# Full attention: the fourth head's first scores a key tile later, peaks of three heads one maximum later

## The reference, cut to what matters

```python
k = jnp.repeat(k, G, axis=2)
v = jnp.repeat(v, G, axis=2)
scale = 1.0 / jnp.sqrt(jnp.float32(HD)).astype(q.dtype)
scores = jnp.einsum('bthd,bshd->btsh', q, k) * scale
probs = jax.nn.softmax(scores, axis=2)
context = jnp.einsum('btsh,bshd->bthd', probs, v).reshape(b, t, DIM)
```

## Time and profile before

| what | value |
|---|---|
| median of 3 runs | 3688.42 us (3686.24 to 3691.95) |
| the profiled execution, its own time | 3693.39 us |
| its span | 3691.6 us |
| PE busy over the span | 3270.0 us (89%) |
| DVE busy | 2747.2 us (74%) |
| ACT busy | 2229.4 us (60%) |
| POOL busy | 954.3 us (26%) |
| first to last score of this stage (line 1824) | 1883.5 to 3299.0 us |

### The profile page before, as it was taken

One profiled execution on the slowest core, in us unless ns is written; L12 is line 12 of the kernel. 1 busy time (PEld: TensorE's weight loads), 2 busy tenths in 40 slices (PEclk: granted clock), 3 DMA queues, 4 the chain that ended last, 5 costly groups with the idle time before them and its releaser, 6 DMA issues. The chain is left out here.

```text
span 3691.6 us, 55325 instructions
## 1 busy us (share of the span) xinstructions
PE 3270.0 (89%) x18162; PEld 1635.2 (44%) x18162; DVE 2747.2 (74%) x4130; ACT 2229.4 (60%) x3970; POOL 954.3 (26%) x906
## 2 busy tenths in 40 slices
PE   7848888997899978996679999999999999977996
PEld 3326777776566646773312222222222222214664
DVE  6639999998566654444688888888888888835665
ACT  5659999998000002221248888888888888862432
POOL 7529999996000000001300000000000000001000
PEclk9979999999899989998879999999999999998998
DMA  4447443321211136313210000000000010011001
GB/s 131 164 139 184 126 104 95 101 58 39 91 54 55 38 68 154 80 46 103 87 25 14 22 14 21 14 21 14 22 14 21 15 24 14 9 34 42 23 23 46
DMA packets 218533, 216.73 MB, mean 59 GB/s; under 512 B 63954, under 2 KB 164434, under 8 KB 217492
## 3 DMA queue, kind: packets, MB, share of 16 engines
q1 hardware_dynamic: 218276, 213.41, 20.9%
HBM read 145.99 MB, written 67.37 MB: 58 GB/s over the span
## 5 line engine op out<-in xcount | busy, mean ns | idle before, releaser
L1720 DVE TENSOR_REDUCE attn_part_max<-attn_pM 128x1 f32<-128x1024 f32 x1024 | 1204.9, 1219 | 161.7 <-PE attn_pM L1775 158.5
L1700 ACT ACTIVATE attn_probs<-attn_pE 128x512 f32<-128x512 f32 x2048 | 1089.8, 597 | 205.4 <-PE attn_pE L1824 200.9
L1824 PE MATMUL attn_pE<-attn_q,attn_k_exp 128*128 128x512 bf16 x2048 | 628.5, 385 | 31.6 <-ACT attn_q L1672 24.7
L535 POOL TENSOR_TENSOR scan_dbu<-scan_du,scan_b_all 128x2048 f32<-128x2048 f32 x128 | 578.2, 4549 | 15.0 <-DVE scan_h L594 13.2
L1795 PE MATMUL attn_pA<-attn_probs,attn_v 128*32 128x512 f32 x4096 | 560.3, 604 | 0.0
L594 DVE TENSOR_TENSOR_SCAN scan_h<-scan_abar,scan_states,scan_dbu 128x512 f32<-128x512 f32 x384 | 458.5, 1290 | 0.0
L1824 PEld LDWEIGHTS attn_pE<-attn_q,attn_k_exp 128*128 128x128 bf16 x2048 | 139.0, 97 | 608.5 <-ACT attn_probs L1700 464.7
L608 PE MATMUL scan_hT<-scan_ident,scan_h 128*128 128x128 f32 x2048 | 327.4, 284 | 68.0 <-ACT scan_hcT L546 26.0
L559 ACT ACTIVATE scan_abar<-scan_delta,scan_decay 128x512 f32<-128x512 f32 x512 | 374.7, 732 | 17.5 <-DVE scan_h L594 17.4
L546 ACT ACTIVATE scan_hcT<-scan_hT,scan_c_t 128x512 f32<-128x512 f32 x512 | 370.0, 723 | 1.2 <-PE scan_hT L608 1.1
L1653 POOL TENSOR_TENSOR attn_peak_parts<-attn_peak,attn_zero 128x4 bf16<-128x4 f32 x128 | 26.3, 205 | 1277.5 <-DVE attn_peak L1724 1277.5
(11 more groups left out here) (274 smaller groups left out, 3637.3 us busy)
## 6 DMA issues: line engine op xcount, KB each, us to landing
scan_b_all<-mid_BC SPq DMA_DIRECT2D x32, 1024.0 KB, 10.3
causal_rwB<-mid_rwT SPq DMA_DIRECT2D x64, 256.0 KB, 4.3
attn_q<-mid_q_parts SPq DMA_DIRECT2D x224, 64.0 KB, 2.4
mid_gT<-front_gT SPq DMA_DIRECT2D x8, 1024.0 KB, 7.6
mid_uT<-front_uT SPq DMA_DIRECT2D x8, 1024.0 KB, 9.2
mid_dT<-front_dT SPq DMA_DIRECT2D x8, 1024.0 KB, 4.3
scan_delta<-mid_dT SPq DMA_DIRECT2D x8, 1024.0 KB, 8.0
scan_u_in<-mid_uT SPq DMA_DIRECT2D x8, 1024.0 KB, 10.4
```

The source lines that it names most:

```text
L535: nc.gpsimd.tensor_tensor(dbu[:, G % NDBU, :, :], du[:, u % 2, :, :], b_row, ALU.mult).then_inc(dbu_ready, 1)
L1700: nc.scalar.activation(probs[:, kt % 4, h, :], pE[:, bank(item), :], ACT.Exp, scale=SCALE).then_inc(exp_done, 1)
L1720: nc.vector.reduce_max(part_max[:, h, j, i:i + 1], pM[:, m % 2, :], AXIS_X).then_inc(max_read, 1)
L1824: nc.tensor.matmul(pE[:, bank(item), :], k_exp[:, par, kt * 128:(kt + 1) * 128], q[:, qc, h, :], start=True, stop=True).then_inc(e_psum, 1)
```

## The change

Two things. First, the item list: head 3's score of tile 0 moves out of tile 0. Tile 0 now has the scores of heads 0 to 2 only; tile 1 has the row of head 3, its own heads 0 to 2, and then head 3 of tile 0 and head 3 of tile 1. In PE's order the sums of tile 14 of the unit before now end tile 0 (they stood in front of the row there as well), the row opens tile 1, and the sums of tile 15 stand in front of the two scores of head 3. The values that semaphores are compared with follow the new order (E_COUNT, KT_COUNT).

Second, DVE takes the peak of heads 0 to 2 not behind the head's last maximum, but behind the first maximum of the next head; the fourth head's stays where it was. A head's first maximum now also waits until the peak of the unit before has been taken (peak_ready), as it overwrites what that reads.

```diff
--- before.py
+++ after.py
@@ -1503,7 +1503,9 @@
     def step_items(kt):
 
         if kt == 0:
-            return [("e", 0), ("e", 1), ("e", 2), ("row", G - 1), ("e", 3)]
+            return [("e", h) for h in range(G - 1)]
+        if kt == 1:
+            return [("row", G - 1)] + [("e", G + h) for h in range(G - 1)] + [("e", G - 1), ("e", 2 * G - 1)]
         items = [("e", kt * G + h) for h in range(G)]
         if kt == OUT_KT:
             items.insert(3, ("out",))
@@ -1513,6 +1515,9 @@
 
     UNIT = [item for kt in range(KT) for item in step_items(kt)]
     P_UNIT = len(UNIT)
+    E_ORDER = [item[1] for item in UNIT if item[0] == "e"]
+    E_COUNT = {e: i + 1 for i, e in enumerate(E_ORDER)}
+    KT_COUNT = [max(E_COUNT[kt * G + h] for h in range(G)) for kt in range(KT)]
     assert P_UNIT % EB == 0
 
     def gone(item, start, end):
@@ -1693,11 +1698,11 @@
                                 if gone(item, start, end):
                                     continue
                                 if item[0] == "e":
-                                    h = item[1] % G
-                                    act.wait_ge(e_psum, u * E_UNIT + item[1] + 1)
+                                    e_kt, h = item[1] // G, item[1] % G
+                                    act.wait_ge(e_psum, u * E_UNIT + E_COUNT[item[1]])
                                     if h == 0:
                                         at_least(act, pv_done, u * KT + kt - 3)
-                                    nc.scalar.activation(probs[:, kt % 4, h, :], pE[:, bank(item), :], ACT.Exp, scale=SCALE).then_inc(exp_done, 1)
+                                    nc.scalar.activation(probs[:, e_kt % 4, h, :], pE[:, bank(item), :], ACT.Exp, scale=SCALE).then_inc(exp_done, 1)
                                 elif item[0] == "row":
                                     move_row(of_unit(item, u), qc if item[1] == G - 1 else (qc + 1) % QC, item[1])
                                 else:
@@ -1717,11 +1722,14 @@
 
                     h, j, i = m // M_HEAD, m % M_HEAD // 2, m % 2
                     dve.wait_ge(m_psum, u * M_UNIT + m + 1)
+                    if j == 0 and i == 0:
+                        at_least(dve, peak_ready, (u - 1) * G + h + 1)
                     nc.vector.reduce_max(part_max[:, h, j, i:i + 1], pM[:, m % 2, :], AXIS_X).then_inc(max_read, 1)
-                    if m % M_HEAD == M_HEAD - 1:
-                        dve.wait_ge(max_read, u * M_UNIT + m + 1)
-                        at_least(dve, parts_ready, (u - 1) * G + h + 1)
-                        nc.vector.tensor_reduce(peak[:, h, :], part_max[:, h, :, :], AXIS_X, ALU.max, negate=True).then_inc(peak_ready, 1)
+
+                def take_peak(h, u):
+                    dve.wait_ge(max_read, u * M_UNIT + (h + 1) * M_HEAD)
+                    at_least(dve, parts_ready, (u - 1) * G + h + 1)
+                    nc.vector.tensor_reduce(peak[:, h, :], part_max[:, h, :, :], AXIS_X, ALU.max, negate=True).then_inc(peak_ready, 1)
 
                 def take_out(u):
                     dve.wait_ge(out_moved, u + 1)
@@ -1736,6 +1744,9 @@
                 nc.vector.tensor_copy(ident_bf[:], ident[:]).then_inc(ident_made, 1)
                 for m in range(M_UNIT):
                     take_max(m, 0)
+                    if m and m % M_HEAD == 0:
+                        take_peak(m // M_HEAD - 1, 0)
+                take_peak(G - 1, 0)
 
                 def body(bg, pair, par, first, last):
                     for qc in range(QC):
@@ -1746,7 +1757,12 @@
                                 take_out(u - 1)
                             if not end:
                                 take_max(2 * kt, u + 1)
+                            if not end and kt and 2 * kt % M_HEAD == 0:
+                                take_peak(2 * kt // M_HEAD - 1, u + 1)
+                            if not end:
                                 take_max(2 * kt + 1, u + 1)
+                            if not end and kt == KT - 1:
+                                take_peak(G - 1, u + 1)
                     if last:
                         take_out(NB * QC - 1)
 
@@ -1761,7 +1777,7 @@
                     if (start and p < 0) or gone(prior, start and p >= 0, end and p >= 0):
                         return
                     if prior[0] == "e":
-                        at_least(pe, exp_done, v * E_UNIT + prior[1] + 1)
+                        at_least(pe, exp_done, v * E_UNIT + E_COUNT[prior[1]])
                     elif prior[0] == "row":
                         at_least(pe, row_moved, of_unit(prior, v) * G + prior[1] + 1)
                     else:
@@ -1788,7 +1804,7 @@
 
                 def sums(u, kt, par):
 
-                    pe.wait_ge(exp_done, u * E_UNIT + kt * G + G)
+                    pe.wait_ge(exp_done, u * E_UNIT + KT_COUNT[kt])
                     if kt == 0:
                         at_least(pe, o_moved, u)
                     for h in range(G):
@@ -1839,17 +1855,16 @@
 
                         for kt in range(KT):
                             items = step_items(kt)
-                            take(items[0])
-                            take(items[1])
+                            pre = 3 if kt == 1 else 2
+                            for item in items[:pre]:
+                                take(item)
                             if not end:
                                 both_maxima(kt)
-                            take(items[2])
-                            if kt == 0 and not start:
-                                sums(u - 1, KT - LAG, par if qc else 1 - par)
-                            for item in items[3:]:
+                            take(items[pre])
+                            if kt < LAG and not start:
+                                sums(u - 1, KT - LAG + kt, par if qc else 1 - par)
+                            for item in items[pre + 1:]:
                                 take(item)
-                            if kt == 1 and not start:
-                                sums(u - 1, KT - 1, par if qc else 1 - par)
                             if kt == LAG:
                                 pe.wait_ge(v_in[par], (pair + 1) * 16)
                             if kt >= LAG:
```

## The result

| | before | changed |
|---|---|---|
| median, first comparison (20 runs each) | 3688.43 us | 3697.11 us |
| ratio | | 1.0022, 95% interval 1.0015 to 1.0029 |
| median, second comparison (15 and 11 runs) | 3691.67 us | 3697.29 us |
| ratio | | 1.0013, 95% interval 1.0004 to 1.0022 |
| the profiled execution, time and span | 3693.39, 3691.6 us | 3695.77, 3694.0 us |

The changed kernel is slower, by 0.22% in the first comparison and 0.13% in the second; the medians differ by 8.7 and 5.6 us. I had said 4.8 us and 3693 us; the median of the first comparison is 3697.11 us, inside the range of 3680 to 3707 us.

The account below looks back on a forecast made before the run. PE, busy 1383 of 1418 us, was taken to set the pace. Order of scores -2.4, peaks +7.5 and lead-in -0.3 made +4.8 us on 3688.4, so 3693 us, range 3680 to 3707.

Parts of the forecast that it names:

- The exchange of waits: Unit's start on PE: the 0.77 us wait for the row's copy goes, bank waits bring 0.77 back; 2.4 us saved.
- e9: Score 9 of a unit, counted from 0, in tile 2: starts at 6.04 and not 5.67, 0.37 us of waiting.
- e11: Score 11 of a unit, counted from 0, in tile 2: starts at 7.52 and not 7.12, 0.40 us more.
- Tile 3: Its first score on PE: 8.83 us after the unit's first score, against 8.96, in units written out.
- e4: Score of tile 1, head 0, behind the row on PE: starts 2.59 us after the unit's first score.
- The peaks: Peaks moved between a tile's two maxima on DVE, where there is no room, delay PE: 7.5 us lost.
- the lower of my two bounds: Price of a peak on DVE that waits for nothing: 0.08 us taken, the upper bound being 0.19.
- the lead-in: Stretch where DVE runs without a pause: gains 3 x 0.11 = 0.3 us from the moved peaks.
- A: Slower rival: the peak costs its whole 0.19 us between the maxima on DVE; +15 us, 3704 us; chance 0.32.
- the rule as I had put it: Skill's rule for DVE: no operation starts before the pipe is empty, and a semaphore after each adds nothing.
- B: Faster rival: the bank waits of tile 2 on PE do not come; 24 us go besides, 3669 us; chance 0.13.
- slower: Outcome of a whole-kernel time above 3695.8 us, rival A and the upper part of the forecast's own terms; chance 0.32.

Follow-up runs that it names:

- experiment 3: Changed kernel with two copies of part_max, so that a head's first maximum needs no second wait: 3689.17 us, ratio 0.9994 to the kernel before.
- experiment 6: Kernel of experiment 5 with ACT's copy of the sums moved ahead of the exponential of head 3, tile 1: 3678.48 us, ratio 0.9961 to before.
- experiment 1: Kernel before with the late peaks alone, scores in the old order: 3699.37 us, ratio 1.0023 to before.
- 2: Kernel before with the new order of scores alone, peaks where they were: 3689.90 us, ratio 1.0004 to before.
- 4: Changed kernel with ACT's copy of the sums ahead of the exponential of head 3, tile 0: 3692.64 us, ratio 1.0006 to before.
- 5: New order with old peaks, head 3's score of tile 0 moved ahead of the sums of tile 15: 3686.74 us, ratio 0.9985 to before.
- 7: Kernel of experiment 6 with two copies of part_max and head 0's peak alone one maximum later: 3673.09 us, ratio 0.9946 to before.

## Why the prediction was right

**The exchange of waits.** Right by mechanism and nearly by size: 0.77 went, e9 and e11 wait instead, each 0.65 to 0.67 behind an exponential as computed. Tile 3 is at 8.90, I had 8.83: e4 comes 0.05 later than taken (2.64 instead of 2.59), as the row adds 0.22 here, where the earlier trace rows had given 0.17. So by the order alone a unit written out gains 0.07 and not 0.13, and one in the loop 0.06 and not 0.03; over 31 units 2.0 us, where 2.4 were forecast. In the changed kernel the start of a loop unit gains nothing (12.02 and 12.03 in the table of experiment 3), as the added wait of tile 0 eats it there. The forecast had 0.03 for the order and 0.02 against it for that wait; the wait costs 0.08.

**The peaks.** Right: a peak that waits for nothing starts 1.14 after the maximum ahead and adds 0.07, the lower of my two bounds, and the second maximum of a tile has no room. Late peaks alone cost 0.13 in a unit written out (0.20 forecast) and 0.25 in the loop (0.28): 6.0 us, where 7.5 less 0.3 in the lead-in were forecast. The places in the loop came out nearly as forecast: tile 5 gains 0.06 (forecast 0.06), tiles 9 and 13 lose 0.14 to 0.15 each (0.16). Two sizes inside these figures were wrong. At tile 5 (the place that I called head 0's first maximum; it is head 1's first, behind which head 0's peak now stands) I had charged no added wait, and it costs 0.09 there, but the gain from the place is 0.16; the two errors cancel. At tile 0 I had charged 0.02, and it costs 0.08 in the new order. The 0.3 us of the lead-in cannot be told: the first division stands at 1940.8 to 1942.4 us in the profiles of before and at 1941.3 and 1941.5 in those of the changed kernel.

**Rivals.** A, the peak's whole price in its new place, would have needed the maximum behind a peak 1.33 after the one ahead; it is 1.21 (2429.39 to 2430.60), and A's time, 15 us or 0.4% more, lies above both intervals. The finding of the Trainium skill that a semaphore after each operation costs nothing extra (VectorE: DVE Perf Modes, The DRAIN you can't avoid; measured there on eight copies) does not carry over to these reductions: the same peak costs 0.19 behind the result it waits for and 0.07 one maximum later. The measurement decides. The other half of the rule as I had put it, that no operation starts before the pipe is empty, left out what that section of the Trainium skill itself adds, that an operation which is not held starts earlier; the maxima that overlap by 0.08 agree with that. B, the whole 0.77 us in each unit, did not come in this kernel; experiment 6 brings 0.55 of it with two more moves.

**The sum.** By the units the change costs 4.9 us by the usual values and 4.1 added up interval by interval; forecast 4.8. That the sum came so close is luck in part: the two parts measured alone, 6.0 us lost and 2.0 won, make 4.0, so the loss was forecast too high, and the 0.07 by which the parts fail to add up in the loop, 1.1 us over 16 units, was in no term of mine. The second comparison gave 0.13%; the first gave 0.22% and leaves 4.9 us (0.13%) just outside its interval. What the rest of the first is stays unsettled. The same gap stands between the units' sum and the ratio of the experiments: 2.5 us in experiment 1, 3.5 in 2, 2.9 in 4, 2.5 in 5, 2.7 in 6, but -1.7 in 3, -0.7 in 7 and 0 in the repeat of the changed kernel. The turn of the loop (3 us) and what lies behind the stage (8.6 us between three profiles of before) vary by as much within one kernel, and with two or three profiles of each no difference between the kernels is shown in either. As for the chances: the median of 3697.11 us lies 1.3 above the 3695.8 that I had set as the bound of "slower", so in the first comparison the outcome with 0.32 came, and in the second the one with 0.55. Both intervals lie above 1, so the change is slower, but not by rival A.

## What to carry to other kernels

With three buffers, taking away one wait is worth only what the next reuse of a buffer allows: count the items that stand in one row behind the longest step, and what stands ahead of the reader on its own engine (here a copy of 0.5 us). An operation on an engine that idles part of the time can still be on the path, as a maximum here whose end frees a buffer. And where waits compare with register values inside a loop, a wait that is always met still has its price (0.08 to 0.09 us here), so a second copy of a small tile can be cheaper than the wait that guards it. Two changes measured alone need not add up: what is hidden beside a wait in one order can cost its full price in the other.

## What was not expected of the hardware

An added wait that is always met costs 0.08 to 0.09 us at each of four places in the loop, where its value comes from a register, and nothing that can be seen in the units written out (44.05 with and without it). I had expected it at two places only. And the turn of the loop: PE stood still for 2.5 to 3.7 us, and in 12 of 13 profiles, whatever the kernel, the granted clock fell to 0.50 there for 3.4 or 6.8 us.
